# Counting edges on one core: one loop per 32 destinations, two edge tiles a pass, instead of one loop per 64 destinations, eight one-hots a pass

## What is computed

```
h  = relu(layernorm(x))
x  = x + gat_gru(h, src, dst)            # softmax over the edges into a node, then a GRU cell
h  = relu(layernorm(x))
for step in range(4):                     # gated graph network
    trans = einsum('nd,tod->tno', h, W_edge) + b_edge
    a     = segment_sum(trans[etype, src], dst)
    h     = gru_cell(a, h)
x  = x + h
```

## Time and profile before

| | us |
|---|---|
| median of three runs | 505.75 (505.05 to 510.2) |
| the profiled execution's own time | 507.11 |
| its span in the trace | 505.3 |
| mean granted TensorE clock | 0.943 of full |

### The profile page before, as it was taken

One profiled execution on the slowest core, in us unless ns is written; L12 is line 12 of the kernel. 1 busy time (PEld: TensorE's weight loads), 2 busy tenths in 40 slices (PEclk: granted clock), 3 DMA queues, 4 the chain that ended last, 5 costly groups with the idle time before them and its releaser, 6 DMA issues.

```text
span 505.3 us, 9333 instructions
## 1 busy us (share of the span) xinstructions
PE 428.2 (85%) x3176; PEld 354.5 (70%) x3176; DVE 289.9 (57%) x746; ACT 174.2 (34%) x310; POOL 12.0 (2%) x33
## 2 busy tenths in 40 slices
PE   1387686688887889587979999999999999999995
PEld 0384354476776678565658788887888878988894
DVE  6979888879889873546544544244442344433322
ACT  3620334556657556344322322023220222212111
POOL 2101000000000000100100000000000000000000
PEclk9869977989889889799999999999999999999998
DMA  6000000000000000000000000000000000000000
GB/s 163 21 0 1 1 1 1 1 1 2 1 2 2 2 2 1 0 1 0 3 5 1 0 1 2 1 0 1 1 1 1 0 2 2 0 1 1 1 22 30
DMA packets 5834, 3.56 MB, mean 7 GB/s; under 512 B 495, under 2 KB 5632, under 8 KB 5788
## 3 DMA queue, kind: packets, MB, share of 16 engines
q1 hardware_dynamic: 4516, 2.42, 1.9%
q10 hardware_dynamic: 1272, 0.54, 0.4%
HBM read 2.31 MB, written 0.64 MB: 6 GB/s over the span
## 4 chain that ended last, share of the span: by engine, by line
PE 69%; DVE 15%; issue 6%; ACT 6%; DVEq 3%; DMA 0%; POOL 0%; SPq 0%; ACTq 0%; POOLq 0%
PE small L1428 34%; PE big L1416 7%; PE big L1284 5%; PE small L1301 5%; DVE cell_hot L837 4%; DVE absent L858 3%; DVE absent L854 3%; ACT absent L455 2%; DVEq L837 2%; PE small L1318 1%; PE big L1379 1%; PE big L1381 1%; PE big L1380 1%; PE big L1370 1%; PE big L1371 1%
## 5 line engine op out<-in xcount | busy, mean ns | idle before, releaser
L1428 PE MATMUL small<-nibbles,store 128*128 128x256 fp8e4 (+1 forms) x1600 | 175.2, 270 | 2.9 <-issue 2.9
L1428 PEld LDWEIGHTS small<-nibbles,store 128*128 128x128 f16 x1600 | 156.1, 98 | 24.2 <-issue 8.3
L1284 PE MATMUL big<-cell_hot,store 128*128 128x320 bf16 x264 | 60.9, 359 | 28.2 <-DVE cell_hot L837 20.2
L837 DVE TENSOR_SCALAR cell_hot<-iota,cell_w,fields 128x320 bf16<-128x320 f16 x264 | 75.2, 357 | 13.8 <-issue 6.6
L1284 PEld LDWEIGHTS big<-cell_hot,store 128*128 x264 | 36.1, 144 | 48.1 <-issue 42.1
L1085 DVE TENSOR_SCALAR aS<-small,edge_down 128x256 f32<-128x256 f32 (+1 forms) x20 | 9.6, 478 | 92.6 <-PE small L1428 92.6
L604 ACT CAST store<-digit_words 128x512 f16<-128x512 f32 x40 | 24.5, 618 | 105.4 <-DVE digit_words L998 105.4
L998 DVE TENSOR_TENSOR digit_words<-big,edge_rows 128x512 f32<-128x512 f32 x40 | 27.1, 689 | 27.5 <-PE big L1416 27.5
L1416 PE MATMUL big<-wT,h 128*128 128x512 f32 x80 | 38.1, 597 | 2.3 <-ACT h L600 2.3
L941 DVE SCALAR_TENSOR_TENSOR cell_hot<-rz,cell_hot 128x256 f32<-128x256 f32 (+1 forms) x25 | 10.5, 419 | 35.9 <-ACT cell_hot L575 35.9
L1301 PE MATMUL small<-ident,nibbles 128*128 128x128 f16 x400 | 29.6, 245 | 0.2
(11 more groups left out here) (241 smaller groups left out, 515.7 us busy)
## 6 DMA issues: line engine op xcount, KB each, us to landing
xn<-in_x SPq DMA_DIRECT2D x1, 576.0 KB
out<-xn SPq DMA_DIRECT2D x4, 128.0 KB
store<-in_edge_attr SPq DMA_DIRECT2D x1, 256.0 KB
wn<-in_L_gnn_W_edge SPq DMA_DIRECT2D x1, 256.0 KB, 6.6
wn<-in_L_gnn_Wi ACTq DMA_DIRECT2D x1, 192.0 KB, 4.0
wn<-in_L_gnn_Wh_g ACTq DMA_DIRECT2D x1, 192.0 KB, 6.5
wn<-in_L_gnn_W_ih SPq DMA_DIRECT2D x1, 192.0 KB, 6.4
wn<-in_L_gnn_W_hh SPq DMA_DIRECT2D x1, 192.0 KB, 6.3
```

The source lines that it names most:

```text
L837: last = v.tensor_scalar(half_hot[:, b * GROUP + q], iota[:, b * HALF:(b + 1) * HALF], cell_w[:, half, bass.ds(tile + q, 1)], fields[:, 1, ...
L1284: last = mm(big[:, 2 * half + b, 0:HALF], lane_hot[:, :, bass.ds(tile + q, 1)].rearrange("p l a -> p (l a)"), half_hot[:, b * GROUP + q], ...
L1428: last = mm((psA, psD)[g % 2][:, 0:w], m16[s % 2][:, i, part, t * P:(t + 1) * P], A8[:, t % 2, i, c * CH:c * CH + w, t // 2], start=(i == ...
```

## The change

Each part of 32 destinations gets its own number of tiles, rounded up to a multiple of 2, and its own loop on DVE and on PE, two tiles a pass: two one-hots, two matmuls, one wait. A window's word now holds two first tiles and two numbers of passes. The one-hots' slot isn't fixed by the place in the pass any more but is the running count of tiles modulo 8, worked out in registers. The eight slots, the one-hots' and the matmuls' shapes, and all that stands between the loops are unchanged. By the inputs above the parts take 13, 6, 5, 4, 4, 3, 3, 3, 3, 3, 3, 3, 2, 3 passes, then 2 each and 1 for the last: 109 passes in 40 loops, 218 one-hots.

```diff
-GROUP = 4
-RING = 2 * GROUP
+GROUP = 2
+RING = 8
...
         def edge_tiles(eng, j, ahead):
-            word = eng.value_load(table[0:1, j:j + 1], min_val=0, max_val=65536 * (ETP + 1))
-            first, second, tiles = eng.snap(word & 255), eng.snap((word >> 8) & 255), eng.snap(word >> 16)
-            return (first, second, tiles, ahead), eng.snap(ahead + 2 * tiles)
+            word = eng.value_load(table[0:1, j:j + 1], min_val=0, max_val=(1 << 24) * (ETP // GROUP + 1))
+            firsts = eng.snap(word & 255), eng.snap((word >> 8) & 255)
+            tiles = eng.snap(((word >> 16) & 255) * GROUP), eng.snap((word >> 24) * GROUP)
+            middle = eng.snap(ahead + tiles[0])
+            return ((firsts[0], tiles[0], ahead), (firsts[1], tiles[1], middle)), eng.snap(middle + tiles[1])
...
+        def ring_slot(before):
+            return nc.s_assert_within(before & (RING - 1), 0, RING - GROUP, skip_runtime_bounds_check_because=
+                                      "the tiles before a group are a multiple of GROUP")
...
             def one_hots(j, half, tiles_of):
-                first, second, tiles, ahead = tiles_of
                 dve.wait_ge(K.cellw, j + 1)
-                dve.sem_inc(K.taken, 1)
-                with dve.Fori(0, tiles, GROUP) as k:
-                    before = dve.snap(ahead + 2 * k)
-                    for b, begin in enumerate((first, second)):
-                        tile = sub_tile(begin, k)
-                        for u in range(0, GROUP, 2):
-                            dve.wait_ge(K.slot, before + b * GROUP + u + 2)
-                            for q in (u, u + 1):
-                                last = v.tensor_scalar(half_hot[:, b * GROUP + q], iota[:, b * HALF:(b + 1) * HALF],
-                                                       cell_w[:, half, bass.ds(tile + q, 1)],
-                                                       fields[:, 1, bass.ds(tile + q, 1)],
-                                                       ALU.is_equal, ALU.mult)
-                            last.then_inc(K.pair, 2)
+                for b, (first, tiles, ahead) in enumerate(tiles_of):
+                    dve.sem_inc(K.taken, 1)
+                    with dve.Fori(0, tiles, GROUP) as k:
+                        before = dve.snap(ahead + k)
+                        tile, slot = sub_tile(first, k), ring_slot(before)
+                        dve.wait_ge(K.slot, before + GROUP)
+                        for q in range(GROUP):
+                            last = v.tensor_scalar(
+                                half_hot[:, bass.ds(slot + q, 1)].rearrange("p a c -> p (a c)"),
+                                iota[:, b * HALF:(b + 1) * HALF],
+                                cell_w[:, half, bass.ds(tile + q, 1)], fields[:, 1, bass.ds(tile + q, 1)],
+                                ALU.is_equal, ALU.mult)
+                        last.then_inc(K.pair, GROUP)
...
-                first, second, tiles, ahead = tiles_of
-                with pe.Fori(0, tiles, GROUP) as k:
-                    before = pe.snap(ahead + 2 * k)
-                    for b, begin in enumerate((first, second)):
-                        tile = sub_tile(begin, k)
-                        for u in range(0, GROUP, 2):
-                            pe.wait_ge(K.pair, before + b * GROUP + u + 2)
-                            for q in (u, u + 1):
-                                last = mm(big[:, 2 * half + b, 0:HALF],
-                                          lane_hot[:, :, bass.ds(tile + q, 1)].rearrange("p l a -> p (l a)"),
-                                          half_hot[:, b * GROUP + q], start=False, stop=False, skip_group_check=True)
-                            last.then_inc(K.slot, 2)
+                for b, (first, tiles, ahead) in enumerate(tiles_of):
+                    with pe.Fori(0, tiles, GROUP) as k:
+                        before = pe.snap(ahead + k)
+                        tile, slot = sub_tile(first, k), ring_slot(before)
+                        pe.wait_ge(K.pair, before + GROUP)
+                        for q in range(GROUP):
+                            last = mm(big[:, 2 * half + b, 0:HALF],
+                                      lane_hot[:, :, bass.ds(tile + q, 1)].rearrange("p l a -> p (l a)"),
+                                      half_hot[:, bass.ds(slot + q, 1)].rearrange("p a c -> p (a c)"),
+                                      start=False, stop=False, skip_group_check=True)
+                        last.then_inc(K.slot, GROUP)
```

More of the change, by code:

```diff
@@ L46 @@
 NS = NP // SUB
-ETP = -(-ET // GROUP) * GROUP
-assert ETP % LANE_PART == 0 and ETP % SLOW == 0
+ETP = -(-ET // LANE_PART) * LANE_PART
+assert ETP % GROUP == 0 and ETP % SLOW == 0
 SLOTS = NW * ETP
@@ L139, in build @@
         best80 = sb("best80", [2 * NS, 1], F32)
-        rg_i = sb("rg_i", [1, 2, NW], I32)
+        rg_i = sb("rg_i", [1, 2, NW, 2], I32)
         rg_f = sb("rg_f", [1, 2, NW, 2], F32)
-        rg_n = sb("rg_n", [1, 3, NW], F32)
+        rg_n = sb("rg_n", [1, 2, NW, 2], F32)
+        rg_w = sb("rg_w", [1, 3, NW], I32)
         table = sb("table", [1, NW], I32)
@@ L790, in _ @@
             up, down = (psB[0:1, q * NS:(q + 1) * NS].rearrange("p (w b) -> p w b", b=2) for q in range(2))
-            begin, tiles_of, room = rg_f[:, 0], rg_n[:, 0], rg_n[:, 1]
+            begin, groups_of, room = rg_f[:, 0], rg_n[:, 0], rg_n[:, 1]
             link(v.tensor_scalar(rg_f[:, 1], down, -1.0, 2.0 * P, ALU.mult, ALU.add))
@@ L794, in _ @@
             link(v.tensor_tensor(rg_f[:, 1], up, begin, ALU.subtract))
[L795 to L802, removed]
+            link(v.tensor_scalar(rg_i[:, 0], rg_f[:, 1], GROUP - 1.0, None, ALU.add))
+            link(v.tensor_scalar(rg_i[:, 1], rg_i[:, 0], 1, None, ALU.logical_shift_right))
+            link(v.tensor_scalar(groups_of, rg_i[:, 1], 1.0, None, ALU.max))
+            v.scalar_tensor_tensor(rg_w[:, 0], groups_of[:, :, 1], 256.0, groups_of[:, :, 0], ALU.mult, ALU.add)
+            link(v.tensor_scalar(room, groups_of, -float(GROUP), float(ETP), ALU.mult, ALU.add))
+            v.tensor_scalar(rg_w[:, 2], rg_w[:, 0], 16, None, ALU.logical_shift_left)
+            link(v.tensor_tensor(begin, begin, room, ALU.min))
+            link(v.scalar_tensor_tensor(rg_w[:, 1], begin[:, :, 1], 256.0, begin[:, :, 0], ALU.mult, ALU.add))
+            v.tensor_tensor(table[:], rg_w[:, 2], rg_w[:, 1], ALU.bitwise_or).then_inc(S0.table, 1)
             dve.wait_ge(S0.fields, 2)
```

## The result

The changed kernel takes **845.45 us** (843.84 to 846.73, four runs), the kernel before beside it 505.96 us (505.05 to 510.2, four runs): a ratio of 1.6681, 95% interval 1.6597 to 1.6766. The forecast was 840 us in a range of 800 to 895.

A forecast was written before the change was run, and what follows sets the result against it. PE's sequencer was taken to bound the changed counting stage: 507.1 + 331 (loops) + 2 (DVE's waits in window 0) + 2 (entries) - 4 (vanished waits) + 4 (clock) = 842 us profiled, forecast 840 us, range 800 to 895.

The forecast's parts named there:

- The pairs: PE's loop bodies: each earlier window adds a REGISTER_ALU and an ISA a pass, 782 x 0.34 = 266 us.
- The 695 us: Whole-kernel forecast if PE's register instructions cost only their shown durations instead of their start-to-start spacings.
- The base: PE's 109 short passes without growing pairs, 1.5 us each in first parts and 1.6 in second: 163 us.
- The sum in the loops: PE's sequencer inside the counting loops: 163 + 266 = 429 us, against 98 before, +331 us.
- Between the loops: Counting stage outside PE's loops: loop entries +2, vanished waits -4, array clock +4 us.
- Entries: 20 added loop entries on PE, 20 x (0.03 + 0.06) = 2 us.
- The edge weights' wait: After window 3, the 3.75 us wait for ACT's scaling should vanish, since PE comes some 30 us later; less 4.
- The array's clock: TensorE, mostly idle in the stage, may run count turns and aggregate at 1.2 GHz: 4 us, bounds 0 to 24.
- the rival with 20 us more: The array's clock is on the path at its upper bound: 842 + 20, 860 us; chance 0.08.
- Jumping back over a long body: PE's jumps over late, longer bodies need fetching anew: 12 to 48 us more, 854 to 890 us; chance 0.12.
- DVE: DVE's loops and work between them take some 220 us, far below PE, so DVE waits for PE.
- Fewer tiles: 264 to 218 one-hots and matmuls: 46 tiles at 0.29 us, 13 us only if tiles were what bounds.

The follow-up runs named there:

- after_kept: The changed kernel with one added PE wait at each window's head, so the sum of earlier tiles stands in a register: 583.38 us, ratio 1.1533 to before.
- after_half: The changed kernel with that added wait at the head of window 10 alone, leaving 392 of 782 pairs: 714.75 us, ratio 1.4095 to before.
- common_two: The kernel before with the sum kept in a register, one loop a window, two tiles of each part a pass, slot by running count: 538.78 us.
- before_kept: The kernel before with an added PE wait at each window's head that keeps the sum in a register: 502.68 us, ratio 0.9928.
- the mask: The kernel before with the word's number of tiles masked with 255 after its shift: 542.61 us, ratio 1.0721.
- later_max: The kernel before with the kept sum, DVE's row_max moved a turn later and weigh behind the turn's second loop: 514.73 us, ratio 1.0161 to before.
- after_four_kept: The changed kernel with four tiles a pass instead of two and the sum kept in a register: 549.25 us, ratio 1.0851 to before.

## Why the prediction was right

**The pairs.** 782 x 0.34 was the deciding term. The trace has 0.347 us in window 19's last pass and 0.344 in its second (19 ALU_OP from 506.9 to 513.1), after_kept and after_half give 0.335 us a pair net. 266 us predicted, 262 measured by taking the pairs away (273 in the loops alone). What made it come out was the spacing. The Trainium skill ("Perfetto Trace Analysis", Sequencer-only Instruction) says that such an instruction shows its execution alone; here 192 + 32 = 224 ns are shown of 347. With the durations in place of the spacings, 183 + 36 ns a pair instead of 340, the prediction's 782 pairs come to 95 us less and the forecast to 745 us, some 100 us too low. The 695 us that the prediction names for this case doesn't follow from the pairs alone, and it doesn't show where the other 50 us are.

**The base.** I had 163 us for 109 passes without pairs, 1.5 and 1.6 us each. after_kept has 154.8 in the loops, and that ends at the last branches' starts; 1.42 us a pass. Window 0 of the changed kernel shows it too, 1.40 us between most of its branches in the first part and 1.59 in the second, where I had 1.5 and 1.6. Some 5% too high.

**The sum in the loops.** 429 predicted, 427.7 measured; before 98, and 100.3. That it comes this close is partly luck: the base was 8 us too high and the pairs, taken in the loops, 7 us too low. The mechanism is right without it, but an agreement within 2 us is better than the terms behind it.

**Between the loops.** I had 2 - 4 + 4 = 2 us: 20 loop entries, the wait for the edge weights, the clock. It is 7.5 us, and the stretches between the loops show how the terms did.

- *Entries.* A MOVE takes 0.09 us to the next instruction, as taken. The 20 new stretches between a window's two loops, from the last branch of one to the MOVE of the other, are 0.13 to 0.18 us each, 2.8 us in all; the last branch itself was in my base.
- *The edge weights' wait* of the earlier trace rows. It is gone from PE's waits, and the stretch after window 3, in which it stood, goes from 4.8 to 1.0 us: 3.8 us less, where I had 4.
- *What is left.* The ten stretches after even windows, which hold the count turns and `aggregate`, grow from 37.8 to 44.0 us, 6.2 us, and the other eight by 2.2 us together. The clock is the nearest reason (next point); I had taken 4 us for it.

**The array's clock.** The stage's granted clock fell from 0.88 to 0.57, mostly the lower of the two levels, 1.2 GHz, after stretches in which two matmuls stand in 1.5 to 8 us. The Trainium skill ("TensorE: Matmul & The Clock Gate", What's actually happening) has the lower level as an idle array's default. The trace agrees, with 0.57 over the stage. The 360 count matmuls of the stage show it, first before, then after:

```profile
L1301 PE MATMUL small<-ident,nibbles 128*128 128x128 f16 x360 | 27.2, 248 | 0.2
```

```profile
L1308 PE MATMUL small<-ident,nibbles 128*128 128x128 f16 x360 | 36.6, 295 | 0.0
```

9.4 us more busy time. The clock's share of what was added between the loops is at most 8.4 us (6.2 and 2.2, above); no run separates it from the rest there. I had taken 4 us, with bounds of 0 to 24; the rival with 20 us more falls. Behind the stage, where I had taken nothing, it is 1.8 us, as much as the same 2175 matmuls are busy longer (294.24 to 296.01 us). The granted clock of the first 5 us there is 0.55, where the kernel before has 1.00.

**Jumping back over a long body.** This rival falls. In windows 18 and 19 the next instruction starts 0.27 to 0.28 us after the branch's start, over bodies of up to 51 instructions; in window 0, over 13, it is 0.27 us in most passes too. None of the 69 jumps back takes longer than 0.32 us, and the longest is in window 0. after_half says the same by its linearity.

**DVE.** As predicted: never the bound in late windows (261.1 us of waiting for PE). But the array still idled 34.8 us for one-hots, against 20.2 before: 31.3 us of it up to 200 us, none behind 300, as PE's line 1290 shows in four stretches (34 to 53, 53 to 110, 110 to 200 and 300 to 400 us):

```profile
L1290 PE MATMUL big<-cell_hot,store 128*128 x26 | 9.2, 445 | 8.1 <-DVE cell_hot L844 5.4 <-issue 2.7
L1290 PE MATMUL big<-cell_hot,store 128*128 x52 | 18.2, 448 | 28.3 <-DVE cell_hot L844 14.5 <-issue 13.8
L1290 PE MATMUL big<-cell_hot,store 128*128 x46 | 17.0, 464 | 56.6 <-issue 45.3 <-DVE cell_hot L844 11.4
L1290 PE MATMUL big<-cell_hot,store 128*128 x28 | 10.4, 467 | 73.2 <-issue 73.2
```

I had counted no such wait after the change, and it grew. It costs next to nothing all the same, since it lies beside the sequencer's own time. after_kept, without the pairs, has 26.6 us of it:

```profile
PE big L1292 <- issue: 46.6, 56, 1.2
...
PE big L1292 <- DVE cell_hot L844: 26.6, 34, 1.1
```

Yet from window 6 on the second passes of its loops take 1.38 to 1.48 us from branch to branch in a first part and 1.51 to 1.56 in a second, as in window 0 (1.40 and 1.58 for most). A wait that held the sequencer up would show there.

**Fewer tiles.** 46 tiles fewer were to be worth nothing in themselves, and no run shows a gain by them: common_two has 24 fewer than before_kept and is 36 us slower. No run changes the number of tiles alone, so what they are worth isn't measured.

**Where I was wrong behind the prediction:** the mask (0.174 us a word, not 0.13, since I had not counted how the operations pack), four tiles a pass (14 us too low, since I took the passes of two tiles for dearer than they are and counted no waits for DVE), and later_max, where I had looked at who waits for the one-hots and not at who waits for `row_max`.

What comes back between the loops whenever the sum is kept is for the most part the sum itself, computed once a window: 10.0 of 11.2 us in after_kept, 10.0 of 10.1 in after_four_kept, 5.7 of 6.9 in before_kept. What stays open is how much of the 8.4 us between the loops is the array's clock, and what a tile less is worth by itself.

## What to carry to other kernels

Before splitting a loop whose length the chip decides, count what the sequencer does in one pass: register arithmetic is paid in every pass, and a running sum that stands in no register grows with every loop before. Look in the built program's order whether a loop's body gets longer from one copy to the next, and give such a value a use ahead of the loop that keeps it in a register. Work saved in tiles is worth nothing if it is bought with more passes, of which each costs the sequencer more than the saved tiles did: here 0.6 to 1.3 us for a further pass.

## What was not expected of the hardware

- A pass of two matmuls with 10 register instructions and a taken branch takes 1.40 us on PE's sequencer in window 0, and 1.42 in the mean of after_kept, where the two matmuls themselves fill 0.7 us. With own loops and four matmuls a pass (after_four_kept) it is 1.9 to 2.0 us. From the two, an estimate: about 0.27 us a tile and 0.9 for the pass itself.
- A register sum's cost is linear to within 1% over 782 pairs (130.7 us for 390, 131.4 for 392), with no surcharge for longer loop bodies.
- One more operation (`& 255`) in a sum costs 36.9 us, as it brings 212 FUSED_REGOPS where 83 were, and only 3.5 us where the sum is kept.
